# A graph attention kernel on one core: a transposed-attribute ring of 8 instead of 3, rings of 3 for the sums, gathered pieces handed back one by one

## The chip, the cores and the metric

The kernel runs on one core of one Trainium2 chip. The metric is the device time of one execution in microseconds. The median of several executions is compared.

## The reference

One graph attention layer (8 heads of 16) with a residual, over 6250 nodes and 206250 edges sorted by destination:

```
h   = relu(layernorm(x))                                  # x [6250, 256]
xm  = h @ W_n2m.T;  ea = edge_attr @ W_r2m.T              # [6250, 128], [206250, 128]
xl  = xm @ Wl.T + bl;  xr = xm @ Wr.T + br
u   = leaky_relu(xl[src] + xr[dst] + ea @ We.T, 0.2)      # one row per edge, and one loop per node
logits = einsum(u as (edge, head, 16), att)
alpha  = softmax of the logits over the edges of one dst
out = segment_sum(xl[src] * alpha, dst) + bias
return x + out @ W_m2n.T
```

A node's loop edge has the mean of its edges' attributes.

## The kernel before, in words

The kernel has three parts. The **prologue** normalises x, writes the table `xl` to HBM, keeps `xr` in SBUF as three bf16 parts, and builds tables on the chip. One of them is `free_tab`: for each entry the value of `msg_ready` at which places of the ring of gathered rows are free again. The **edge loop** is what the change is about. The **finale** adds the loop edges, divides by the sums and projects.

The edges are cut into 806 pieces of 256. A step takes two pieces (512 edges), and there are 427 steps, since a piece that crosses a window of 128 nodes is walked twice. All engines walk the same steps, each in its own order, and meet by semaphores alone. Logits, maxima and weights are made for batches of 8 steps, so that the weighted sums of a step (its aggregation) come `LAG = 18` steps behind its logits. In iteration k:

- **SP** issues `slot_bc` for step k+2 (L777), reads the step's piece numbers from a table (L101), issues two `attrT` DMAs for step k (transposed attributes, 32 rows by 512 edges, L786), then two `rbf` DMAs for step k-17 (L794). Before `attrT` it waits for `z_done` of step k-TRING, before `slot_bc` for the one-hot of step k-2, before `rbf` for the copy of four steps earlier. Once in a batch it issues masks (L768).
- **GpSimd** gathers `xl` rows by source into `xl_g`, a ring of 64 pieces, two gathers per piece (L811). From piece 64 on it waits once per `FREED = 2` pieces on `msg_ready` against a value of `free_tab`.
- **TensorE** makes z of step k in one PSUM bank of two: six matmuls with the one-hot of destinations (L832), the attributes (L836, contraction over 32 rows), four transposes of the gathered rows (L840). Then the logits of step k-2 (L867), the aggregation of step k-18 (L881, `onehot` by `msg`) and, once a batch, transposes for maxima (L850, L856) and weights (L891). z of step k waits until u of step k-2 is made.
- **ScalarE** copies gathered rows to `xl_z` for step k+2 (L905), makes `onehot` of step k-17 (L927, L932), copies `rbf` into `msg` (L936), and makes the relu of z (L943).
- **VectorE** makes the one-hot of step k+2 (L983), `msg` of step k-17 (L1005 and L1010, which also signal `msg_ready`), adds the aggregation of step k-19 into `acc` (L1022, L1024), and makes u of step k (L1027). Its scans for the maxima follow in some iterations.

`onehot` and `msg` have two places each. So ScalarE's L932 and VectorE's L1005 of iteration k wait for `agg_done` of TensorE's iteration k-1. VectorE's L1022, behind L1005 in the same iteration, waits for that same aggregation.

Of the kernel before, what the change touches and what calls it, by code (L numbers as in the profile page):

```python
# [10 lines left out]
P = 128  # L11
# [3 lines left out]
TILES = 4  # L15
# [21 lines left out]
SRING = 4  # L37
TRING = 3
ARING = 4
PRING = 64  # L40
ZRING = 3
FREED = 2
FREE_ROW = 4
MRING = 2
UNROLL = 48
BATCH = 8
# [41 lines left out]
def inside(j, count):  # L88

    return not isinstance(j, int) or 0 <= j < count  # L90
# [92 lines left out]
def prologue(nc, banks, xl_table, slot_dram, masks_dram, inputs,  # L183
# [5 lines left out]
    with ExitStack() as ctx:  # L189
# [89 lines left out]
        col_ps = banks[:, 7, WALK // 2:WALK // 2 + CHUNKS * SPLIT]  # L279
        free_ps = banks[0:1, 3, 0:FREES]  # L280
        tab_ps = [banks[:, i].rearrange("p (t r) -> p t r", t=TILES) for i in range(2)]
# [178 lines left out]
        def _(pe):  # L460
# [24 lines left out]
            pe.wait_ge(met_ready, 1)  # L485
            nc.tensor.matmul(free_ps, ones[0:WINDOWS, 0:1], met[:], start=True, stop=True).then_inc(met_counted, 1)

# [24 lines left out]
            pe.wait_ge(tab_copied, CHUNKS)  # L512
            pe.wait_ge(free_ready, 1)
            for w, s, _ in sweep(pe, -1, WRING, WINDOWS - 2, WINDOWS, WRING, WRING):
# [18 lines left out]
        def _(dve):  # L533
# [64 lines left out]
            for to in (loads[:, 0:STEPS, 0:SPLIT], loads[:, LATE:, SPLIT:], by_step[:, 0:STEPS], sums[:, 0:STEPS, SPLIT:]):  # L598
                nc.vector.tensor_scalar(to, pieces[:, 0:STEPS], float(PIECES - 1), None, ALU.min).then_inc(tabs_ready, 1)
            dve.wait_ge(met_counted, 1)  # L600
            nc.vector.scalar_tensor_tensor(out=free_tab, in0=free_ps, scalar=TICK / SPLIT, in1=free_base[:],
                                           op0=ALU.mult, op1=ALU.add).then_inc(free_ready, 1)

# [57 lines left out]
def edge_loop(nc, banks, xl_table, slot_dram, masks_dram, attr_rows, attr_cols,  # L661
# [11 lines left out]
    with ExitStack() as ctx:  # L673
        def sb(name, shape, dt=FP32):
            return ctx.enter_context(nc.sbuf_tensor(name, shape, dt))
# [6 lines left out]
        masks = sb("masks", [P, MRING, MASKS], BF16)  # L682
        attrT = sb("attrT", [D_RBF, TRING, GROUP])
        xl_g = sb("xl_g", [P, PRING, PT, D_MSG])
# [3 lines left out]
        distance = sb("distance", [P, TILES, P])  # L688
        onehot = sb("onehot", [P, 2, TILES, P])
        msg = sb("msg", [P, 2, TILES, AGG])  # L690
        run_ends = sb("run_ends", [P, 4])
# [67 lines left out]
        def _(sp):  # L759
            for k, s, r in sweep(sp, -2, 4 * BATCH, STEPS - 2, STEPS + LATE, UNROLL, UNROLL):  # L760
# [21 lines left out]
                if inside(k, STEPS):  # L782
                    if inside(k - TRING, STEPS):
                        sp.wait_ge(z_done, k - TRING + 1)
                    for h in range(SPLIT):
                        sp.dma_start(attrT[:, s % TRING, h * PIECE:(h + 1) * PIECE],  # L786
                                     attr_cols[one(now[h])].rearrange("a k e -> (a k) e")
                                     ).then_inc(turned_in[s % TRING], 16)
# [31 lines left out]
        def _(pe):  # L820
            pe.wait_ge(set_up, SET_UP)
            for k, s, r in sweep(pe, first, *looped, last_turn, UNROLL, UNROLL):
                if inside(k, STEPS):
# [11 lines left out]
                    pe.wait_ge(turned_in[s % TRING], (r * (UNROLL // TRING) + s // TRING + 1) * FULL)  # L835
                    nc.tensor.matmul(z, Wc[0:D_RBF], attrT[:, s % TRING], start=False, stop=False)  # L836
                    pe.wait_ge(xl_ready, SPLIT * (k + 1))
# [33 lines left out]
                if inside(k - LAG, STEPS):  # L871
                    j = s - LAG
                    pe.wait_ge(msg_ready, TICK * (k - LAG + 1))
                    pe.wait_ge(attr_ready, TICK * (k - LAG + 1))
                    pe.wait_ge(oh_ready, TICK * (k - LAG + 1))
                    if inside(k - LAG - 2, STEPS):
                        pe.wait_ge(added, TICK * (k - LAG - 1))
                    for h in range(SPLIT):
                        for i in range(PT):
                            t = h * PT + i  # L880
                            mm = nc.tensor.matmul(U_ps[j % 2][:, h], onehot[:, j % 2, t], msg[:, j % 2, t],  # L881
                                                  start=i == 0, stop=i == PT - 1)
                    mm.then_inc(agg_done, 1)
# [14 lines left out]
        def _(act):  # L898
            for k, s, r in sweep(act, first, *looped, last_turn, UNROLL, UNROLL):
# [23 lines left out]
                if inside(k - LAG + 1, STEPS):  # L923
# [5 lines left out]
                    act.wait_ge(dist_ready, TILES * (k - LAG + 2))  # L929
                    if inside(k - LAG - 1, STEPS):  # L930
                        act.wait_ge(agg_done, k - LAG)
                    nc.scalar.activation(onehot[:, m % 2], distance[:], ACT.Relu, scale=-1.0, bias=1.0  # L932
                                         ).then_inc(oh_ready, TICK)
                if inside(k - LAG + 1, STEPS):
                    act.wait_ge(loads[m % ARING], (r * (UNROLL // ARING) + (s - LAG + 1) // ARING + 1) * FULL)
                    nc.scalar.activation(msg[:, m % 2, :, CNT:AGG],  # L936
                                         rbf[:, m % ARING].rearrange("p (t k) -> p t k", t=TILES), ACT.Copy
                                         ).then_inc(attr_ready, TICK)
# [22 lines left out]
        def _(dve):  # L961
# [5 lines left out]
            for k, s, r in sweep(dve, first, *looped, last_turn, UNROLL, UNROLL):  # L967
# [27 lines left out]
                if inside(k - LAG + 1, STEPS):  # L995
                    row = slice(m % BATCH * HEADS, (m % BATCH + 1) * HEADS)
                    if m % BATCH == 0:
                        b = r * (UNROLL // BATCH) + (s - LAG + 1) // BATCH
                        dve.wait_ge(wT_done, b + 1)
                    if inside(k - LAG - 1, STEPS):  # L1000
                        dve.wait_ge(agg_done, k - LAG)
                    to = msg[:, m % 2, :, 0:MSG].rearrange("p t (h c) -> p t h c", c=HC)
                    for h in range(SPLIT):
# [432 lines left out]
```

## Time and profile before

| | |
|---|---|
| median of 3 runs | 3236.71 us (3231.31 to 3242.29) |
| the profiled execution's own time | 3200.59 us |
| its span | 3198.8 us |
| busy share of the span: TensorE, VectorE, ScalarE, GpSimd | 78%, 46%, 49%, 51% |
| mean granted clock of TensorE | 0.828 |

The span runs from the first to the last instruction. "PE" is TensorE's matmuls, "PEld" its weight loads, "DVE" VectorE, "ACT" ScalarE, "POOL" GpSimd, "SPq" the queue of SyncE, which only issues DMAs. "issue" names idle time that ends with nothing that the profile shows, and "remote" a semaphore whose updater it cannot tell. The granted clock is 1.0 at 2.4 GHz and 0.5 at 1.2 GHz.

### The profile page before, as it was taken

The page shows a single profiled execution, that of the slowest core. Times are in us where ns is not written, and L with a number is a line of the kernel's source. Part 1 is how long each engine was busy: PE and PEld are TensorE (multiplying, and loading weights), DVE is VectorE, ACT ScalarE, POOL GpSimd, SP SyncE. Part 2 cuts the span into 40 slices and gives each one's busy share as a digit, 9 for nine tenths or more (in the row PEclk, how much of TensorE's full clock was granted, in tenths as well). Part 3 has the DMA queues.
Part 4 walks back from the last instruction along what each step waited for, and adds up shares of the span by engine and source line. Part 5 has one row for each costly group of instructions (what it writes and reads, how often), then busy time and mean ns, then how long its engine had stood idle before and what let it go on. Part 6 is the DMA issues. An engine that isn't in the chain of part 4 may idle for free. (4 is left out here: it accounts for less than half of the span.)

```text
span 3198.8 us, 62156 instructions
## 1 busy us (share of the span) xinstructions
PE 2501.8 (78%) x11639; PEld 1541.6 (48%) x11640; DVE 1470.5 (46%) x4279; ACT 1552.9 (49%) x4428; POOL 1631.7 (51%) x1819
## 2 busy tenths in 40 slices
PE   5613878888788888888887888878888878887987
PEld 3401545545455555445454555445554545444565
DVE  6401444444444444445444444444444444444577
ACT  3301545555455445445545455554545544544672
POOL 4874455555455455555555455555555555555203
PEclk9755988888888888878888788888888887888999
DMA  4221333333333333333333333333333333333317
GB/s 144 83 56 48 85 79 82 85 81 83 81 81 79 84 85 82 82 82 87 82 79 88 85 81 79 85 79 77 85 83 91 86 78 85 82 82 78 78 30 132
DMA packets 317109, 263.45 MB, mean 82 GB/s; under 512 B 173619, under 2 KB 289637, under 8 KB 316438
## 3 DMA queue, kind: packets, MB, share of 16 engines
q1 hardware_dynamic: 254222, 142.33, 17.1%
q0 software_dynamic: 57632, 113.02, 14.7%
q10 hardware_dynamic: 4840, 3.68, 0.4%
q8 instruction: 124, 2.03, 0.3%
q14 instruction: 291, 2.38, 0.3%
HBM read 247.39 MB, written 16.89 MB: 83 GB/s over the span
## 5 line engine op out<-in xcount | busy, mean ns | idle before, releaser
L811 POOL DMA_INDIRECT xl_g<-xl_table,src_tab x1612 | 1532.5, 951 | 1353.8 <-DVE msg L1010 871.7
L881 PE MATMUL banks<-msg,onehot 128*128 128x177 f32 x3416 | 771.9, 375 | 58.0 <-issue 51.7
L881 PEld LDWEIGHTS banks<-msg,onehot 128*128 128x128 f32 x3416 | 633.7, 226 | 265.7 <-issue 235.4
L1027 DVE SCALAR_TENSOR_TENSOR uT<-banks,uT 128x512 f32<-128x512 f32 x427 | 294.4, 689 | 922.1 <-ACT uT L943 480.5
L836 PE MATMUL banks<-attrT,Wc 32*128 32x512 f32 x854 | 548.2, 724 | 145.0 <-DMA attrT<-in_attr_cols 117.2
L927 ACT ACTIVATE distance<-iota_n,minus_slot 128x128 f32<-128x128 f32 x1708 | 550.4, 388 | 119.4 <-issue 119.1
L1005 DVE TENSOR_TENSOR msg<-xl_g,banks 128x256 f32<-128x256 f32 x854 | 320.8, 417 | 571.5 <-remote 409.6
L832 PE MATMUL banks<-onehotT,xr_parts 128*128 128x256 bf16 x2562 | 419.6, 303 | 196.1 <-issue 168.4
L943 ACT ACTIVATE uT<-banks 128x512 f32<-128x512 f32 x427 | 249.7, 585 | 648.4 <-remote 445.3
L905 ACT ACTIVATE xl_z<-xl_g 128x256 f32 x854 | 310.9, 407 | 224.2 <-issue 162.0
L932 ACT ACTIVATE onehot<-distance 128x512 f32<-128x512 f32 x427 | 269.0, 630 | 299.1 <-remote 164.1
L832 PEld LDWEIGHTS banks<-onehotT,xr_parts 128*128 x2562 | 270.3, 107 | 285.7 <-issue 217.8
L840 PEld LDWEIGHTS banks<-ident,xl_z 128*128 128x128 f32 x1708 | 203.2, 155 | 409.5 <-issue 363.3
L867 PE MATMUL banks<-uT,att_pad 128*64 128x256 f32 x1708 | 345.7, 474 | 31.2 <-issue 29.8
L840 PE MATMUL banks<-ident,xl_z 128*128 128x128 f32 x1708 | 320.8, 315 | 33.9 <-issue 33.0
L836 PEld LDWEIGHTS banks<-attrT,Wc 32*128 32x128 f32 x854 | 141.6, 206 | 262.1 <-DMA attrT<-in_attr_cols 136.2
L983 DVE TENSOR_SCALAR onehotT<-slot_bc,node_of 128x512 bf16<-128x512 bf16 x427 | 152.8, 358 | 81.9 <-issue 68.6
L1024 DVE TENSOR_TENSOR acc<-acc,banks 128x177 f32 x427 | 145.1, 340 | 73.6 <-issue 13.0
L867 PEld LDWEIGHTS banks<-uT,att_pad 128*64 128x64 f32 x1708 | 100.1, 153 | 120.9 <-issue 118.4
L1022 DVE TENSOR_TENSOR acc<-acc,banks 128x177 f32 x427 | 140.8, 330 | 5.2 <-issue 3.8
L936 ACT ACTIVATE msg<-rbf 128x128 f32<-128x128 f32 x427 | 126.5, 296 | 31.6 <-DMA rbf<-in_attr_rows 18.6
L856 PE MATMUL banks<-ones,end_row 1*128 1x1 f32 x216 | 40.8, 289 | 83.8 <-DVE end_row L1059 64.2
(199 smaller groups left out, 1430.3 us busy)
## 6 DMA issues: line engine op xcount, KB each, us to landing
slot_bc<-slot_dram SPq DMA_DIRECT2D x427, 128.0 KB
attrT<-in_attr_cols SPq DMA_DIRECT2D x854, 32.0 KB
rbf<-in_attr_rows SPq DMA_DIRECT2D x854, 32.0 KB
xl_g<-xl_table,src_tab POOLq DMA_INDIRECT x1612
masks<-masks_dram SPq DMA_DIRECT2D x108, 96.5 KB
out<-in_x SPq DMA_DIRECT2D x16, 336.0 KB
out<-result POOLq DMA_DIRECT2D x6, 896.0 KB, 8.4
xl_table<-lr_sb SPq DMA_DIRECT2D x49, 64.0 KB, 1.5
```

The lines of the kernel that those rows point to most:

```text
L811: pool.indirect_dma_start(out=xl_g[:, g % PRING, i], out_offset=None, in_=xl_table, in_offset=bass.IndirectOffsetOnAxis(ap=src_tab[:, j:j ...
L832: nc.tensor.matmul(z[:, h * PIECE:(h + 1) * PIECE], parts_of(xr_parts, w[h], part), onehotT[:, n4, h * PIECE:(h + 1) * PIECE], start=h == ...
L836: nc.tensor.matmul(z, Wc[0:D_RBF], attrT[:, s % TRING], start=False, stop=False)
L840: mm = nc.tensor.matmul(z[:, h * PIECE + i:(h + 1) * PIECE:PT], xl_z[:, s % ZRING, h, i], ident[:], start=False, stop=h == SPLIT - 1 and i ...
L867: mm = nc.tensor.matmul(LT_ps[par][h * ROWS:(h + 1) * ROWS], att_pad[:, ROWS - HEADS - i * HEADS:2 * ROWS - HEADS - i * HEADS], uT[:, n, h ...
L881: mm = nc.tensor.matmul(U_ps[j % 2][:, h], onehot[:, j % 2, t], msg[:, j % 2, t], start=i == 0, stop=i == PT - 1)
L905: nc.scalar.activation(xl_z[:, (s + 2) % ZRING, h].rearrange("p i d -> p (i d)"), xl_g[:, one(pieces[h] & (PRING - 1))].rearrange("p a i d ...
L927: nc.scalar.activation(distance[:, t], iota_n[:], ACT.Abs, bias=minus_slot[:, one(TILES * (k - LAG + 1) + t)]).then_inc(dist_ready, 1)
L932: nc.scalar.activation(onehot[:, m % 2], distance[:], ACT.Relu, scale=-1.0, bias=1.0).then_inc(oh_ready, TICK)
L943: nc.scalar.activation(uT[:, s % URING], z_ps[s % 2], ACT.Relu, scale=1.0 - SLOPE).then_inc(relu_ready, 1)
L1005: nc.vector.tensor_tensor(to[:, two, :, 0:D_HEAD], xl_g[:, one(pieces[h] & (PRING - 1))].rearrange("p a i (h d) -> p (a i) h d", d=D_HEAD) ...
L1027: nc.vector.scalar_tensor_tensor(out=uT[:, s % URING], in0=z_ps[s % 2], scalar=SLOPE, in1=uT[:, s % URING], op0=ALU.mult, op1=ALU.add).the ...
```

## The change

Three things change in the edge loop, and one in the prologue follows from them.

- `attrT` has 8 places instead of 3. They lie four to a column range, on 32 partitions each, so L836 takes its operands from partitions 0, 32, 64 or 96 on, with a tile position to match. `Wc` holds the same weights four times already.
- `onehot` and `msg` have 3 places instead of 2: L932 and L1005 wait for the aggregation one iteration earlier than before.
- `FREED` is 1: GpSimd waits and counts per piece, and reads four entries of `free_tab` per 4 pieces instead of per 8.
- `free_tab` so has 808 entries instead of 404: its count is made by two matmuls into two banks and two VectorE operations, and the comparison `met` is twice as wide.

```
-TRING = 3
+TRING = 8
+TROWS = P // D_RBF
...
-FREED = 2
+FREED = 1
...
+SUM_RING = 3
...
-        free_ps = banks[0:1, 3, 0:FREES]
+        free_ps = banks[0:1, 2:4, 0:FREES // 2]
...
-            nc.tensor.matmul(free_ps, ones[0:WINDOWS, 0:1], met[:], start=True, stop=True).then_inc(met_counted, 1)
+            for i in (0, 1):
+                nc.tensor.matmul(free_ps[:, i], ones[0:WINDOWS, 0:1], met[:, i * (FREES // 2):(i + 1) * (FREES // 2)],
+                                 start=True, stop=True).then_inc(met_counted, 1)
...
-            dve.wait_ge(met_counted, 1)
-            nc.vector.scalar_tensor_tensor(out=free_tab, in0=free_ps, scalar=TICK / SPLIT, in1=free_base[:],
-                                           op0=ALU.mult, op1=ALU.add).then_inc(free_ready, 1)
+            for i in (0, 1):
+                half = slice(i * (FREES // 2), (i + 1) * (FREES // 2))
+                dve.wait_ge(met_counted, i + 1)
+                nc.vector.scalar_tensor_tensor(out=free_tab[:, half], in0=free_ps[:, i], scalar=TICK / SPLIT,
+                                               in1=free_base[:, half], op0=ALU.mult, op1=ALU.add).then_inc(free_ready, 1)
...
-        attrT = sb("attrT", [D_RBF, TRING, GROUP])
+        attrT = sb("attrT", [P, TRING // TROWS, GROUP])
...
-        onehot = sb("onehot", [P, 2, TILES, P])
-        msg = sb("msg", [P, 2, TILES, AGG])
+        onehot = sb("onehot", [P, SUM_RING, TILES, P])
+        msg = sb("msg", [P, SUM_RING, TILES, AGG])
...
+                    to = slice(s % TROWS * D_RBF, (s % TROWS + 1) * D_RBF)
                     for h in range(SPLIT):
-                        sp.dma_start(attrT[:, s % TRING, h * PIECE:(h + 1) * PIECE],
+                        sp.dma_start(attrT[to, s % TRING // TROWS, h * PIECE:(h + 1) * PIECE],
...
-                    nc.tensor.matmul(z, Wc[0:D_RBF], attrT[:, s % TRING], start=False, stop=False)
+                    of = slice(s % TROWS * D_RBF, (s % TROWS + 1) * D_RBF)
+                    nc.tensor.matmul(z, Wc[of], attrT[of, s % TRING // TROWS], start=False, stop=False,
+                                     tile_position=(s % TROWS * D_RBF, 0))
...
-                    if inside(k - LAG - 1, STEPS):
-                        act.wait_ge(agg_done, k - LAG)
-                    nc.scalar.activation(onehot[:, m % 2], distance[:], ACT.Relu, scale=-1.0, bias=1.0
+                    if inside(k - LAG + 1 - SUM_RING, STEPS):
+                        act.wait_ge(agg_done, k - LAG + 2 - SUM_RING)
+                    nc.scalar.activation(onehot[:, m % SUM_RING], distance[:], ACT.Relu, scale=-1.0, bias=1.0
...
-                    if inside(k - LAG - 1, STEPS):
-                        dve.wait_ge(agg_done, k - LAG)
-                    to = msg[:, m % 2, :, 0:MSG].rearrange("p t (h c) -> p t h c", c=HC)
+                    if inside(k - LAG + 1 - SUM_RING, STEPS):
+                        dve.wait_ge(agg_done, k - LAG + 2 - SUM_RING)
+                    to = msg[:, m % SUM_RING, :, 0:MSG].rearrange("p t (h c) -> p t h c", c=HC)
```

## Rows read from the trace of the kernel before

**Rows 1.** The page: busy us, share of the span and instructions of each engine.

```profile
PE 2501.8 (78%) x11639; PEld 1541.6 (48%) x11640; DVE 1470.5 (46%) x4279; ACT 1552.9 (49%) x4428; POOL 1631.7 (51%) x1819
```

**Rows 2.** Windows by stage: us, busy and instructions per engine, clock, DMA share, GB/s.

```profile
110.00:300.00 190.00, 44.66 (x126) 19.92 (x124) 16.97 (x37) 11.24 (x27) 132.58 (x148) 0.52 0.23 59
...
400.00:2950.00 2550.00, 2089.81 (x9688) 1275.48 (x9685) 1163.80 (x3431) 1299.13 (x3760) 1345.02 (x1420) 0.83 0.33 82
```

**Rows 3.** Waits of TensorE, 400 to 2950 us: total us, times, longest.

```profile
PE banks L836 <- DMA attrT<-in_attr_cols: 117.2, 42, 11.1
...
PE banks L856 <- DVE end_row L1059: 58.9, 14, 6.5
...
PE banks L891 <- DVE msg L1010: 38.7, 21, 4.7
```

**Rows 4.** Waits of SyncE's queue, 400 to 2950 us.

```profile
SPq L786 <- remote: 62.6, 14, 10.1
SPq L786 <- PE banks L840: 16.0, 6, 6.3
SPq L794 <- ACT msg L936: 1.1, 1, 1.1
SPq L777 <- DVE onehotT L983: 0.3, 2, 0.2
```

**Rows 5.** Timeline of a late `attrT`: start us, us, engine, line, what.

```profile
1739.31 0.01 SPq L777 DMA_DIRECT2D slot_bc<-slot_dram  x1
...
1742.04 0.33 SPq L777 DMA_DIRECT2D slot_bc<-slot_dram  x1
...
1754.36 0.34 SPq L777 DMA_DIRECT2D slot_bc<-slot_dram  x1
...
1755.50 0.86 SPq L786 DMA_DIRECT2D attrT<-in_attr_cols  x2
...
1758.06 2.07 PE L836 MATMUL banks<-attrT,Wc 32*128 32x512 f32 x2 [3.87 <-DMA attrT<-in_attr_cols]
```

**Rows 6.** Timeline, same stretch: first and last of a run of 8 gathers, and next.

```profile
1741.20 0.94 POOL L811 DMA_INDIRECT xl_g<-xl_table,src_tab  x1 [3.48 <-DVE msg L1010]
...
1749.93 0.94 POOL L811 DMA_INDIRECT xl_g<-xl_table,src_tab  x1 [0.30 <-issue]
...
1754.55 0.94 POOL L811 DMA_INDIRECT xl_g<-xl_table,src_tab  x1 [3.67 <-DVE msg L1010]
```

**Rows 7.** Waits of GpSimd, 400 to 2950 us.

```profile
POOL xl_g L811 <- DVE msg L1010: 780.7, 184, 11.4
```

**Rows 8.** Waits of VectorE before `msg`, 400 to 2950 us.

```profile
DVE msg L1005 <- remote: 383.3, 96, 6.7
```

**Rows 9.** Timeline while GpSimd fills its ring: a relu long after its z.

```profile
157.55 1.12 PE L840 MATMUL banks<-ident,xl_z 128*128 128x128 f32 x4
...
184.78 0.60 ACT L943 ACTIVATE uT<-banks 128x512 f32<-128x512 f32 x1 [26.17 <-remote]
```

**Rows 10.** Timeline: two steps of TensorE at the full clock.

```profile
1512.71 1.47 PE L881 MATMUL banks<-msg,onehot 128*128 128x177 f32 x8
...
1514.02 0.82 PE L832 MATMUL banks<-onehotT,xr_parts 128*128 128x256 bf16 x6
...
1514.77 1.12 PE L836 MATMUL banks<-attrT,Wc 32*128 32x512 f32 x2
...
1515.82 0.66 PE L840 MATMUL banks<-ident,xl_z 128*128 128x128 f32 x4
...
1516.98 1.47 PE L881 MATMUL banks<-msg,onehot 128*128 128x177 f32 x8
```

**Rows 11.** Timeline of the prologue: the table of free places.

```profile
28.69 1.50 PE L486 MATMUL banks<-met,ones 49*1 49x404 f32 x2
...
32.86 3.67 DVE L599 TENSOR_SCALAR tabs<-walk 1x854 int32<-1x854 f32 x4
...
36.57 0.57 DVE L601 SCALAR_TENSOR_TENSOR tabs<-banks,free_base 1x404 int32<-1x404 f32 x1
```

More of the change, by code:

```diff
@@ L512, in _ @@
             pe.wait_ge(tab_copied, CHUNKS)
-            pe.wait_ge(free_ready, 1)
+            pe.wait_ge(free_ready, 2)
             for w, s, _ in sweep(pe, -1, WRING, WINDOWS - 2, WINDOWS, WRING, WRING):
@@ L880, in _ @@
                             t = h * PT + i
-                            mm = nc.tensor.matmul(U_ps[j % 2][:, h], onehot[:, j % 2, t], msg[:, j % 2, t],
+                            mm = nc.tensor.matmul(U_ps[j % 2][:, h], onehot[:, j % SUM_RING, t], msg[:, j % SUM_RING, t],
                                                   start=i == 0, stop=i == PT - 1)
@@ L935, in _ @@
                     act.wait_ge(loads[m % ARING], (r * (UNROLL // ARING) + (s - LAG + 1) // ARING + 1) * FULL)
-                    nc.scalar.activation(msg[:, m % 2, :, CNT:AGG],
+                    nc.scalar.activation(msg[:, m % SUM_RING, :, CNT:AGG],
                                          rbf[:, m % ARING].rearrange("p (t k) -> p t k", t=TILES), ACT.Copy
```

## The prediction

> **What bounds the kernel now.** I read the page first. TensorE is busiest at 78%, and nothing else passes 51% [rows 1]. The windows then split the time. The stretch from 400 to 2950 us, the steady edge loop, is 2550 of the 3198.8 us: TensorE is busy 2089.81 us there at a granted clock of 0.83, and GpSimd 1345.02 us [rows 2]. With 6.78 us per step (2550 us over about 376 steps, which are the 1420 gathers of that row by 3.775 per step: 1612 over 427) this is where a ring can matter.
>
> TensorE is not a plain bound. It idles 460 us there (2550 less 2089.81). The waits say for what. The largest is the one this change aims at: 117.2 us in 42 waits for `attrT` at L836. Behind it come 58.9 us for VectorE's scans (L856) and 38.7 us for `msg` (L891) [rows 3]. Clock 0.83 between two levels, 0.5 and 1.0, means that a third of the time TensorE runs at 1.2 GHz.
>
> So why is `attrT` late? If the ring of 3 were the reason, SP would stand at L786 until a place came free. It does so 20 times, for 62.6 + 16.0 = 78.6 us, and waits for nothing else (1.4 us) [rows 4]. The rest of its 2550 us SP is passing instructions, and the timeline shows at what pace. From one `slot_bc` to the next it takes 2.73 us when GpSimd is quiet (1739.31 to 1742.04), but 12.32 us (1742.04 to 1754.36, with a pair of mask loads in it) when GpSimd issues a run of eight gathers [rows 5, 6]. After that one the `attrT` of the stalled step is issued at 1755.50 and L836 starts at 1758.06, 3.87 us late [rows 5]. Gathers at 1.25 us each (0.94 and 0.30 between, [rows 6]) are 3.775 x 1.25 = 4.7 us of each step. SP does 4.7/12.3 = 0.38 of a step in them, and the other 0.62 takes 0.62 x 2.73 = 1.7 us: 6.4 us, next to the 6.78 us of a step. SP has hardly any slack. A longer ring can give it only the time in which it now stands, not a faster pace.
>
> GpSimd itself is not the bound: 780.7 us it waits for VectorE to free places [rows 7]. But its runs of gathers hold up others. While it fills its ring (110 to 300 us), TensorE is busy 44.66 of 190 us [rows 2], and a z that ends at 158.67 is taken up by ScalarE only at 184.78, after 26.17 us of "remote" [rows 9]. In the steady loop the same shows as VectorE's 383.3 us of "remote" before `msg` [rows 8]: TensorE's signal reaches it late.
>
> **The change part by part.**
>
> *attrT ring of 8.* It removes the wait at L786, up to 78.6 us of SP's time [rows 4]. What is late next: SP of iteration k then waits for the one-hot of step k-2 (L777) and the copy of `rbf` four steps back. These let it run about four steps ahead instead of two, so six of the eight places serve nobody. TensorE gets back from its 117.2 us [rows 3] no more than SP gains, since both sides are one queue: the stall comes where SP's lead is zero, the wait where it is two. Lower bound: nothing (at the late `attrT` in [rows 5] SP was behind by its own pace, not by the ring). Upper bound: 78.6 us. With a lead that wanders between 0 and 4 instead of 0 and 2, the ends are met about half as often. I take half: -39 us. The number of DMAs, of waits and of SP's instructions per step stays the same.
>
> *L836 in four row groups.* Two matmuls of 0.5 us and two weight loads per step, as before, over 32 rows. Cost taken: 0. The Trainium skill, TensorEngine Tiling (Array Packing), Key Properties, speaks against it: changing the tiling mode drains TensorE. By that rule, if the explicit tile position is a mode that L836 was not in, the matmul before and the one behind would each be waited out. What the rows show on either side: L832 ends at 1514.84 while L836 starts at 1514.77, and L836 ends at 1515.89 while L840 starts at 1515.82 [rows 10]. So there is 0.07 us of overlap on each side to lose: 0.14 x 427 = 60 us at most.
>
> *onehot and msg rings of 3.* L1005 no longer waits for the aggregation of iteration k-1, on which 383.3 us [rows 8] stand. But L1022, next on VectorE, waits for the same one, so the idle time moves behind `msg` and does not vanish. What becomes earlier is `msg`, hence `msg_ready`, by about the 1 us that L1005 and L1010 take: for TensorE's L891, which waits 38.7 us in 21 waits, at most 21 us, and for L856, 14 waits [rows 3], at most 14 us. ScalarE's L932 likewise stands before its L943. Behind it SP's `rbf` wait is already 1.1 us [rows 4]. Since SP has no slack to follow a faster TensorE, I take 0 of these 35 us and keep them as the range's lower side.
>
> *FREED of 1.* GpSimd waits on 742 pieces instead of 371 pairs and reads its table twice as often. The sequencer is ahead of the gathers within a run, where they stay 0.30 us apart [rows 6], so these instructions are hidden by the 0.94 us of a gather. If that cover were gone, 371 more waits at such a gap of 0.30 us would be 111 us, and GpSimd has 780.7 us of waiting to take them from [rows 7]. The two pieces of a step are freed by L1005 and L1010 within half a microsecond, and GpSimd needs 2.5 us per piece. It gives neither time nor more even runs: 0.
>
> *Prologue.* One more pair of matmuls (1.50 us), one more L601 (0.57 us), and a `met` twice as wide (404 columns more, by L599's 0.92 us for 854: 0.4 us) [rows 11]. Together 2.5 us, partly under other work on both engines; I take +2 us, with 0 and 2.5 as bounds.
>
> Sum: -39 + 0 + 0 + 0 + 2 = -37 us on the profiled execution's 3200.59 us, a factor of 0.9884. The median of the runs shown is 1.1% above that execution. The factor on the median, 3236.71, gives **3199 us**. Its own range, from 0 to -78.6 - 35 us: 3122 to 3239.
>
> **The rivals.**
>
> *The lead is not what SP lacks.* SP is late by its pace. The 20 waits give their time back and it is lost at the next late signal, because L777 ties SP to VectorE, which itself waits for TensorE's late signals. For it: [rows 5], where a place was free long before 1755.50. Against it: 78.6 us are real. It gives -9 to +9 us, 3228 to 3246, say 3238.
>
> *Longer runs of gathers (the other side).* `msg` now goes out before the wait for the aggregation. So places come free while TensorE's signal is still held back, GpSimd adds four gathers (5.0 us) to the run, and the signal is held back for as long. TensorE can go on for two steps only, by its two z banks: 2 x 4.27 us at the full clock (L881 at 1512.71 and 1516.98 [rows 10]). The run of 8 gathers, 10 us, just exceeds that; one of 12 stalls it another 5 us. The ring's 37 us are used up when 8 of the 1420/8 = 178 runs get longer (8 x 5 = 40). With 18 of them it is 90 - 37 = +53 us, a factor of 1.0166: 3290. I take the middle of 3246 and 3290, about 3270. For it: [rows 9], where a relu stands 26 us behind its z in an unbroken run. Against it: four gathers per step are freed whatever the order, so longer runs must also be rarer.
>
> *The stalls took the clock with them.* If the 42 stalls vanish, so does the slow clock behind them. A step at 1.2 GHz has L836 at 2.07 us against 1.12 [rows 5, 10], so by that ratio its 4.27 us grow by 3.6 us. 117.2 + 42 x 3.6 = 268 us less, a factor of 0.916: 2966; with half the stalls gone, 3101. The Trainium skill, TensorE: Matmul & The Clock Gate, says that the slow clock is the idle state and sustained activity releases it; clock 0.83 at 82% busy [rows 2] agrees. Against it: SP must supply the steps.
>
> *A drain at every L836.* +60 us by the rows above, less the 37 gained: +23 us, 3260; without the gain 3297.
>
> **How the numbers follow.** Forecast (a gain of 0.3 to 2.5%) 0.43; clock comes back too 0.09; no lead gained 0.23; longer runs 0.21; drain 0.04. A measurement of this kernel tells 0.3%, 10 us, from no change. Faster 0.43 + 0.09 = 0.52, less what of the forecast's own range lies within 10 us, 0.02: 0.50. Same 0.23 + 0.02 = 0.25. Slower 0.21 + 0.04 = 0.25. The range ends at 3120 on the fast side, at the forecast's own lower bound and short of the clock rival's 3101, and at 3272 on the slow side, so that the longer-runs rival is in it up to its middle. What is left out is some 0.09 and 0.11.
>
> **What would show it.** Right: the `attrT` wait at L836 falls from 117.2 to about 60 us; SP's waits at L786 are gone, and short ones appear at L777; VectorE's idle time moves from L1005 to L1022; L891's wait shrinks; L836 starts no later after L832. No lead gained: the `attrT` wait stays near 117 us. Longer runs: GpSimd shows runs of 12 and more, and TensorE waits at L832 for u. Clock: granted clock over 0.87 in the loop. The prediction is wrong if SP's pace is no property of the gathers but of its own waiting, or if VectorE's earlier `msg` changes the rhythm of the gathers.

## The result and the profile after

The change is slower: 3365.76 us median (3341.29 to 3372.72, 4 runs) against 3234.01 us (3206.04 to 3242.29, 4 runs: the three shown above and one more), a ratio of 1.0404 with a 95% interval of [1.0362, 1.0445]. The forecast was 3199 us, with a range from 3120 to 3272. The profiled execution has a span of 3361.9 us, 163.1 us more than before.

The page's first line of the kernel after, engines and busy time, against [rows 1]:

```profile
PE 2572.0 (77%) x11641; PEld 1569.3 (47%) x11642; DVE 1468.0 (44%) x4280; ACT 1553.4 (46%) x4428; POOL 1633.4 (49%) x1819
```

VectorE, ScalarE and GpSimd are busy for as long as before, within 3 us, so they only wait longer. TensorE is busy 70 us more for the same instructions, at a lower granted clock. The windows of the kernel after, against [rows 2]:

```profile
110.00:300.00 190.00, 45.41 (x129) 20.49 (x128) 17.04 (x37) 11.38 (x28) 132.81 (x150) 0.52 0.22 60
...
400.00:2950.00 2550.00, 2036.08 (x9140) 1230.47 (x9140) 1095.42 (x3237) 1226.71 (x3548) 1267.87 (x1337) 0.81 0.30 78
```

In equal time GpSimd issues 1337 gathers in place of 1420: a step takes 7.20 us, not 6.78. Nothing changed while the ring fills (45.41 against 44.66 us). So the loss is in the steady loop. Its waits, kernel after (line numbers moved: L832 is now L839, L836 L844, L840 L849, L856 L865, L881 L890, L891 L900; L1005 and L1010 are L1014 and L1019, L1022 L1031, L1027 L1036; L943 is L952, L811 L818; L768 L774, L777 L783, L794 L801. In the experiments below they lie a few lines off too, and the name of what is written says which is meant):

```profile
PE banks L839 <- issue: 156.0, 95, 3.2
PE banks L865 <- DVE end_row L1068: 75.7, 25, 6.4
...
PE banks L900 <- DVE msg L1019: 44.7, 23, 2.9
...
DVE uT L1036 <- ACT uT L952: 684.6, 165, 9.1
DVE acc L1031 <- remote: 301.3, 37, 11.6
...
DVE msg L1014 <- remote: 51.4, 12, 5.8
...
ACT uT L952 <- remote: 560.2, 92, 9.5
...
POOL xl_g L818 <- DVE msg L1019: 897.7, 169, 8.7
...
SPq L774 <- DVE run_max L1088: 27.6, 16, 2.3
SPq L783 <- DVE onehotT L992: 23.4, 23, 2.7
SPq L801 <- ACT msg L945: 0.2, 1, 0.2
```

Three things are to be seen. The wait that the forecast lived on, L836 for `attrT` [rows 3], is no longer among the waits, nor is SyncE's for a place [rows 4]. VectorE no longer stands at `msg` (383.3 us of "remote" in [rows 8], now 51.4) but at `acc` (301.3) and at uT (684.6, before 407.2 as shown below). And GpSimd waits 897.7 us for `msg`, 117 us more than in [rows 7]. The line of the kernel before, VectorE's waits, 400 to 2950 us:

```profile
DVE uT L1027 <- ACT uT L943: 407.2, 109, 9.7
```

One cycle shows how these hang together. Timeline of the kernel after, all engines in order of time:

```profile
1735.34 0.94 POOL L818 DMA_INDIRECT xl_g<-xl_table,src_tab  x1 [5.70 <-DVE msg L1019]
...
1740.82 2.73 PE L890 MATMUL banks<-msg,onehot 128*128 128x177 f32 x8
...
1741.50 0.22 DVE L1019 COPY msg<-banks 128x64 f32<-128x64 f32 x1
...
1745.36 0.66 PE L849 MATMUL banks<-ident,xl_z 128*128 128x128 f32 x4
...
1749.23 0.95 POOL L818 DMA_INDIRECT xl_g<-xl_table,src_tab  x1 [0.30 <-issue]
...
1752.81 0.60 ACT L952 ACTIVATE uT<-banks 128x512 f32<-128x512 f32 x1 [7.76 <-remote]
1752.89 0.34 DVE L1031 TENSOR_TENSOR acc<-acc,banks 128x177 f32 x1 [11.16 <-remote]
...
1753.63 0.69 DVE L1036 SCALAR_TENSOR_TENSOR uT<-banks,uT 128x512 f32<-128x512 f32 x1
...
1756.83 0.75 DVE L1014 TENSOR_TENSOR msg<-xl_g,banks 128x256 f32<-128x256 f32 x2
...
1757.49 0.23 DVE L1019 COPY msg<-banks 128x64 f32<-128x64 f32 x1
...
1758.02 0.95 POOL L818 DMA_INDIRECT xl_g<-xl_table,src_tab  x1 [7.85 <-DVE msg L1019]
```

A run of 12 gathers lasts from 1735.34 to 1750.18. TensorE ends an aggregation at 1743.55 and a z at 1746.02, but both signals reach VectorE and ScalarE at 1752.8, 2.7 us after the run. The trace has the updates of these two semaphores themselves at 1752.67 and 1752.79 us. So it is the signals that are late, and not the engines that wait for them. VectorE has already written the next `msg` (L1019 at 1741.50) and stands at `acc`. Before GpSimd can start again, VectorE must do `acc`, uT, the work of a batch, the one-hot and the next `msg`: 7.85 us without a gather. In [rows 6] that gap is 3.67 us, with VectorE standing at `msg` itself.

The Trainium skill, Perfetto Trace Analysis, Per-instruction lifecycle, says that the propagation of a semaphore lies outside the recorded slices. This trace agrees: no row holds the 6.8 us from the end of L849 to L952, it appears as "remote" alone.

### The profile page after: what moved, and what is told of

Its sections match the earlier page's. It is cut to its first block and busy times, and to the rows that moved or that the text cites. A ratio compares the mean times of both kernels' runs of the same rounds, so it can differ in the third digit from the quotient of the medians.

```text
span 3361.9 us, 62601 instructions
## 1 busy us (share of the span) xinstructions
PE 2572.0 (77%) x11641; PEld 1569.3 (47%) x11642; DVE 1468.0 (44%) x4280; ACT 1553.4 (46%) x4428; POOL 1633.4 (49%) x1819
## 5 line engine op out<-in xcount | busy, mean ns | idle before, releaser
L818 POOL DMA_INDIRECT xl_g<-xl_table,src_tab x1612 | 1533.9, 952 | 1514.5 <-DVE msg L1019 1054.7
L890 PE MATMUL banks<-msg,onehot 128*128 128x177 f32 x3416 | 788.3, 380 | 88.1 <-issue 83.1
L1036 DVE SCALAR_TENSOR_TENSOR uT<-banks,uT 128x512 f32<-128x512 f32 x427 | 294.6, 690 | 1136.4 <-ACT uT L952 805.6
L890 PEld LDWEIGHTS banks<-msg,onehot 128*128 128x128 f32 x3416 | 644.4, 229 | 295.0 <-issue 245.3
L952 ACT ACTIVATE uT<-banks 128x512 f32<-128x512 f32 x427 | 250.4, 586 | 1053.2 <-remote 772.3
L839 PE MATMUL banks<-onehotT,xr_parts 128*128 128x256 bf16 x2562 | 441.6, 309 | 297.2 <-issue 277.9
L844 PE MATMUL banks<-attrT,Wc 32*128 32x512 f32 x854 | 559.5, 736 | 42.8 <-issue 42.7
L839 PEld LDWEIGHTS banks<-onehotT,xr_parts 128*128 x2562 | 276.3, 109 | 406.7 <-issue 333.1
L849 PEld LDWEIGHTS banks<-ident,xl_z 128*128 128x128 f32 x1708 | 206.8, 157 | 428.9 <-issue 356.7
L876 PE MATMUL banks<-uT,att_pad 128*64 128x256 f32 x1708 | 357.0, 477 | 46.0 <-issue 45.6
L849 PE MATMUL banks<-ident,xl_z 128*128 128x128 f32 x1708 | 327.6, 319 | 40.8 <-issue 29.9
L1031 DVE TENSOR_TENSOR acc<-acc,banks 128x177 f32 x427 | 142.0, 333 | 483.5 <-remote 350.8
L1014 DVE TENSOR_TENSOR msg<-xl_g,banks 128x256 f32<-128x256 f32 x854 | 320.7, 416 | 59.9 <-remote 53.0
L844 PEld LDWEIGHTS banks<-attrT,Wc 32*128 32x128 f32 x854 | 144.0, 208 | 160.0 <-issue 153.8
L865 PE MATMUL banks<-ones,end_row 1*128 1x1 f32 x216 | 45.8, 312 | 99.5 <-DVE end_row L1068 92.0
```

What stands on the lines that cost most here:

```text
L818: pool.indirect_dma_start(out=xl_g[:, g % PRING, i], out_offset=None, in_=xl_table, in_offset=bass.IndirectOffsetOnAxis(ap=src_tab[:, j:j ...
L839: nc.tensor.matmul(z[:, h * PIECE:(h + 1) * PIECE], parts_of(xr_parts, w[h], part), onehotT[:, n4, h * PIECE:(h + 1) * PIECE], start=h == ...
L844: nc.tensor.matmul(z, Wc[of], attrT[of, s % TRING // TROWS], start=False, stop=False, tile_position=(s % TROWS * D_RBF, 0))
L849: mm = nc.tensor.matmul(z[:, h * PIECE + i:(h + 1) * PIECE:PT], xl_z[:, s % ZRING, h, i], ident[:], start=False, stop=h == SPLIT - 1 and i ...
L876: mm = nc.tensor.matmul(LT_ps[par][h * ROWS:(h + 1) * ROWS], att_pad[:, ROWS - HEADS - i * HEADS:2 * ROWS - HEADS - i * HEADS], uT[:, n, h ...
L890: mm = nc.tensor.matmul(U_ps[j % 2][:, h], onehot[:, j % SUM_RING, t], msg[:, j % SUM_RING, t], start=i == 0, stop=i == PT - 1)
```

## The experiments

All kernels below have one addition: the numbers read from tables are ANDed (`& 2047`, `& 1023`) before GpSimd and ScalarE wait on them. The kernel before that each ratio compares with has no AND. `m_before` is the kernel before with that alone. The theories:

- **A, the gate.** The rings of 3 let `msg` go out before VectorE waits for the aggregation. That changes when GpSimd's runs start, and carries the whole loss.
- **B, SyncE.** The ring of 8 lets SyncE run far ahead, and its transfers or its waits in another order cost the time.
- **C, single pieces.** Giving back piece by piece costs GpSimd time.

### The parts one by one

The kernel before on this chip: 3233.49 us.

`m_before`: 3246.99 us, 1.0032 [0.9999, 1.0066].

> The kernel before, where each value read from a table is bounded by an AND with a constant (2047 for msg_ready, 1023 for landed) before it is waited for; the experiments that follow have the same ANDs. One register operation more per step on ScalarE, one per piece pair on GpSimd: all theories expect within 0.3% of before.

`m_ring8`: `TRING = 8` with its row groups, alone.

> The attrT ring of 8 alone. Theory A (the earlier msg changes the rhythm of the gathers and carries the whole loss of 4.0%): 0 to 1.2% faster than before. Theory B (SP far ahead carries it: its DMAs then go out beside the gathers, and TensorE's signals reach ScalarE later): 3 to 4% slower, and ScalarE's remote wait at its relu, 336.4 us before and 598.7 us after, is up here too. Theory C (handing back single pieces): as A here.

Measured: 3244.68 us, 1.0025 [0.9982, 1.0069]. `m_sum3`: `SUM_RING = 3` with the earlier waits of VectorE and ScalarE, alone.

> The rings of 3 for onehot and msg alone. Theory A: 3 to 4% slower, with runs of 12 gathers more often. Theories B and C: within 0.5% of before, with VectorE's idle time moved from L1005 to L1022.

Measured: 3414.49 us, 1.0536 [1.0482, 1.0591]. `m_freed1`: `FREED = 1` with its prologue, alone.

> The pieces handed back one by one alone, with the table for it. Theory C: 3 to 4% slower. Theories A and B: within 0.3% of before, 2 us of prologue.

Measured: 3222.38 us, 0.9965 [0.9931, 0.9999]. As single causes B and C fall, and the rings of 3 alone lose at least as much as the whole change (5.4% against 4.0%, and against 4.5% for the same change measured again below). What gives the difference back is open: neither the ring of 8 nor the single pieces were run on top of the rings of 3 alone. With rings of 3 alone SyncE comes to stand for a place. Windows and SyncE's waits of `m_sum3`, 400 to 2950 us:

```profile
400.00:2950.00 2550.00, 2033.74 (x8982) 1222.86 (x8980) 1075.17 (x3174) 1206.44 (x3480) 1243.37 (x1316) 0.79 0.30 76
...
SPq L787 <- remote: 165.5, 45, 10.3
SPq L787 <- PE banks L841: 85.2, 26, 11.4
```

These 250.7 us cost TensorE nothing directly: in `m_sum3`, with its `attrT` ring of 3, none of TensorE's waits is for `attrT`. So the wait of [rows 3] goes away without the ring of 8.

With the ring of 8 alone SyncE hardly waits for a place, and L836 waits for `attrT` as much as before. ScalarE's "remote" wait at its relu, which theory B expected to rise, is 223.8 us against 258.9 in `m_before`. (Of the two values in the expectation 598.7 is up to 3100 us; up to 2950 us it is 560.2.) The same stretch of `m_before`, then of `m_ring8`:

```profile
PE banks L836 <- DMA attrT<-in_attr_cols: 192.0, 72, 7.6
...
SPq L786 <- remote: 20.8, 4, 10.0
SPq L786 <- PE banks L840: 11.3, 3, 8.1
```

```profile
PE banks L839 <- DMA attrT<-in_attr_cols: 183.8, 74, 9.3
...
SPq L788 <- remote: 0.7, 1, 0.7
```

### Which wait, and is it GpSimd's start?

The kernel before on this chip: 3229.23 us. `s3_dve_old` has rings of 3, with this edit in VectorE's stream:

```
-                    if inside(k - LAG + 1 - SUM_RING, STEPS):
-                        dve.wait_ge(agg_done, k - LAG + 2 - SUM_RING)
+                    if inside(k - LAG - 1, STEPS):
+                        dve.wait_ge(agg_done, k - LAG)
```

> Rings of 3 for onehot and msg, but VectorE still waits for the previous aggregation before it writes msg, as before the change; only ScalarE's earlier wait before onehot is used. Against the kernel with rings of 3 alone, 3414 us. The gate theory: the loss comes from msg_ready being raised, and GpSimd's next run of gathers started, while TensorE's signals are still under way; with VectorE's old wait the next run starts as before, so the loss is gone: 3225 to 3265 us, the waits of ScalarE's relu for TensorE in all 400 to 2950 us back near 420 us, GpSimd's gathers near 1400 in that stretch. The rival, that ScalarE's earlier onehot puts ScalarE in another order against its relu: the loss stays, 3380 to 3420 us. A second rival, that a third buffer costs by its place in memory alone: the loss stays too.

Measured: 3247.44 us, 1.0112 [1.0012, 1.0213]. `s3_act_old` is the same edit in ScalarE's stream instead.

> The mirror of the kernel before it: rings of 3, ScalarE keeps the old wait for the previous aggregation before onehot, VectorE alone writes msg early. The gate theory: the whole loss stays, 3385 to 3425 us, with GpSimd's runs as in rings of 3 alone. The rival of ScalarE's order: the loss is gone, 3225 to 3265 us. If each of the two kernels carries a part, both theories have a share and the parts are read from the two ratios.

Measured: 3419.46 us, 1.0624 [1.0535, 1.0714]. So VectorE's early `msg` is the carrier. ScalarE's early one-hot and the third buffer as such are not, though the interval of `s3_dve_old` leaves them up to 2.1%; `s3_added`, which keeps both, is at 1.0058. `s3_added` has both early waits, and at GpSimd

```
-                    pool.wait_ge(msg_ready, freed[g // FREED % FREE_ROW] & 2047)
+                    pool.wait_ge(added, freed[g // FREED % FREE_ROW] & 2047)
```

> Rings of 3 and both early waits, and one word changed at GpSimd: before it reuses a piece it waits for `added` (VectorE's two additions to acc, which follow the aggregation) in place of msg_ready, with the same counts. The ring of 64 pieces holds 16 steps more than the piece in use, so nothing is held back for want of a buffer beyond one step. The gate theory: GpSimd's runs start again behind TensorE's signal, and the loss is gone, 3210 to 3265 us, though msg is still early. The rival of ScalarE's order, and the rival of the third buffer's place in memory: 3380 to 3420 us. A third possibility, that a gate one step later leaves the piece ring short: over 3300 us with ScalarE waiting for landed.

Measured: 3239.96 us, 1.0058 [1.0016, 1.0099]. `msg` is as early as in `m_sum3`, only GpSimd starts behind the aggregation again, and 5% of loss become 0.6%. The same count of `added` comes two iterations after that of msg_ready, since VectorE adds step k-19 where it makes `msg` of step k-17. That leaves GpSimd no shorter of room: ScalarE waits 33.1 us for gathered rows in `s3_added` and 51.7 us in `m_before`. Waits of `s3_added`, 400 to 2950 us:

```profile
PE banks L837 <- DMA attrT<-in_attr_cols: 189.8, 83, 6.9
...
POOL xl_g L812 <- DVE acc L1025: 809.4, 189, 13.6
...
DVE acc L1023 <- remote: 390.6, 85, 7.0
```

VectorE stands at `acc` as long as in `m_sum3` (385.5 us), so it is not that wait which costs, but what lies between it and GpSimd's next start. And as the loss goes, TensorE's `attrT` wait returns: 189.8 us, near the 192.0 of `m_before`. `b_added` is the kernel before with the same one word.

> The kernel before with rings of 2 and the same one word: GpSimd waits for `added` in place of msg_ready, so a run of gathers starts one operation of VectorE later (after the two additions, some 1.5 us behind msg). The gate theory in its strong form: what matters is how much of TensorE's and VectorE's chain lies between two runs, so this is 0 to 2% faster than before, 3170 to 3245 us. In its weak form (what matters is only that the run starts behind the aggregation's signal, and it does already): within 0.5% of before, 3225 to 3255 us. If GpSimd's own pace sets the step, 1.5 us later per step cannot be caught up: slower, 3280 us and more.

Measured: 3287.08 us, 1.0215 [1.0117, 1.0313]. Neither form of the theory was right: later is not better. The size is that of the third case. From VectorE's place at `msg` the two additions to `acc` now lie before GpSimd's start as well, and the gap that follows a stall there is 4.34 us in place of 3.58 (table below).

The account of all these comes from the gather records between 400 and 2950 us. Gathers less than 0.6 us apart are one run. The time per gather, times 1612, splits into that within runs and that between them. The last columns say at which of VectorE's instructions a run's end finds it, and the mean gap that follows:

```
kernel        runs  in runs   in gaps   span    at msg       at uT        at acc
before         212  1947 us    951 us   3198.8  114, 3.30 us  67, 5.44 us    0
m_before       221  1946       991      3228.8  125, 3.58     55, 5.27       5, 1.64 us
m_ring8        220  1944       994      3240.9  131, 3.64     48, 5.53       0
m_freed1       241  1941       974      3223.4
s3_dve_old     214  1951       972      3227.2  118, 3.47     55, 5.61       0
s3_added       212  1956       981      3237.7   21, 3.57     38, 5.31     110, 3.78
b_added        206  1962      1009      3279.2  121, 4.34     38, 5.38       3, 2.91
after          194  1951      1122      3361.9   29, 1.87     98, 5.55      37, 6.99
change_again   199  1943      1170      3394.9
s3_act_old     187  1949      1181      3416.7   27, 1.55     91, 5.76      37, 8.07
m_sum3         189  1945      1182      3415.5   29, 1.71     75, 5.81      47, 7.74
```

The time within runs is the same everywhere, within 21 us. So the gaps must grow with the span, which is arithmetic and proves nothing yet: 951 to 1122 is +171 us where the span grows by 163.1, and within one chip 991 (`m_before`) to 1182 (`m_sum3`) is +191 where it grows by 186.7. What tells the cause is the last columns. A run's end used to find VectorE at `msg`, 3.3 us from the next gather, in more than half of the cases. With the early `msg` it mostly finds it at uT or at `acc`, 5.5 to 8 us away.

Longer runs are not the main cost. Behind a run of 8 gathers the mean gap is 4.43 us in the kernel before, 5.27 in the one after and 5.82 in `m_sum3`; behind one of 12 it is 6.86, 7.38 and 8.03 us. Per gather a run of 12 has about as much gap as one of 8 (0.57 and 0.55 us in the kernel before). It is the gap behind runs of equal length that grew.

### Without the gathers, and on another chip

`plain_b` and `plain_s3` replace the gather of the edge loop:

```
-                pool.indirect_dma_start(out=xl_g[:, g % PRING, i], out_offset=None, in_=xl_table,
-                                        in_offset=bass.IndirectOffsetOnAxis(ap=src_tab[:, j:j + 1], axis=0),
-                                        engine_sem=landed).then_inc(landings[j % FLIGHT], 16)
+                pool.dma_start(xl_g[:, g % PRING, i], xl_table[0:P]).then_inc(landings[j % FLIGHT], 16)
+                pool.sem_inc(landed, 1)
```

These two and `t8f1` and `all_added` ran on a chip on which the kernel before itself took 2293.43 us (2290.75 to 2299.24), not 3230.

> The kernel before, with each of the 1708 indirect gathers replaced by an ordinary DMA of the same 64 KB from 128 fixed rows of the table, issued by GpSimd at the same place under the same waits. It leaves out the gather itself: the rows are the wrong ones, so its output is not the reference's; all other work is the same. All theories: GpSimd is no longer busy 0.95 us per piece, TensorE's signals are not held back, and the time falls to between TensorE's busy time of 2572 us with its issue gaps and 2950 us. If it stays above 3100 us, the gathers were never what lengthens the step, and the gate theory falls as a whole.

Measured: 2200.0 us median, 0.9593 [0.9577, 0.9609], from four runs of 2199.33 to 2205.00 us. A fifth, the one with the trace, took 4903.28 us with TensorE busy 99% of its span. Why is open, and nothing here rests on that trace.

> Rings of 3 for onehot and msg, with the same replacement of the gathers as in the kernel before it, and the same part of the work left out. The gate theory: without gathers there is nothing to start too early, so rings of 3 cost nothing: within 0.5% of plain_b, or up to 2% faster, since VectorE may run ahead. The rival, that the third ring costs by itself (order of VectorE and ScalarE, place of the buffers in memory): 4 to 6% slower than plain_b, as rings of 3 were against before.

Measured: 2195.46 us (2194.56 to 2196.58), 0.9566 [0.9552, 0.9581]: rings of 3 cost nothing without the indirect gathers. But this chip can't say that the gathers were the reason, since the loss of the rings of 3 was never shown on it. `t8f1` is the whole change without rings of 3.

> The whole change without rings of 3: attrT as a ring of 8 in four row groups, and pieces given back one by one. Single pieces alone measured 0.9965 and the ring of 8 alone 1.0025 against the kernel before. If they add, 0.996 to 1.001, 3215 to 3240 us. If the ring of 8 is worth something only when the runs of gathers are shorter (SyncE then is held less), 0.985 to 0.995. If the three parts only lose together, about 1.00.

Measured: 2294.93 us, 1.0004 [0.9995, 1.0013]. `all_added` is the whole change with GpSimd waiting for `added`.

> The whole change with one word more: GpSimd waits for `added` in place of msg_ready before it reuses a piece. The gate theory: the change's loss of 4% is gone, and it stands as rings of 3 with the same wait (1.0058) plus what single pieces give: 0.998 to 1.010, 3225 to 3262 us. If the loss of the whole change has another cause than that of rings of 3 alone, it stays above 1.02.

Measured: 2291.70 us, 0.9988 [0.9979, 0.9997]. The sizes expected were for the other kind of chip. Here nothing distinguishes the kernels, and the trace says why. Timeline of `t8f1` while GpSimd fills its ring, against [rows 9]:

```profile
186.55 0.94 POOL L817 DMA_INDIRECT xl_g<-xl_table,src_tab  x1 [0.30 <-issue]
...
186.57 0.66 PE L848 MATMUL banks<-ident,xl_z 128*128 128x128 f32 x4
187.13 0.58 ACT L951 ACTIVATE uT<-banks 128x512 f32<-128x512 f32 x1
...
187.80 0.94 POOL L817 DMA_INDIRECT xl_g<-xl_table,src_tab  x1 [0.30 <-issue]
```

Within an equally unbroken run of equally long gathers the relu starts as its z ends. In [rows 9] it starts 26 us later. From 110 to 2050 us of `t8f1` 134 relus found ScalarE idle, and none of them started more than 0.12 us behind its z. Windows of `t8f1`:

```profile
110.00:300.00 190.00, 154.33 (x676) 81.08 (x675) 77.96 (x205) 75.85 (x217) 144.43 (x161) 0.76 0.41 103
400.00:2050.00 1650.00, 1610.17 (x8994) 1017.49 (x8992) 1088.83 (x3186) 1197.92 (x3497) 1248.20 (x1319) 0.98 0.47 118
```

TensorE is busy 154.33 of 190 us while the ring fills (44.66 in [rows 2]), and 98% of the steady loop at a granted clock of 0.98. It is the bound, so the start of a run should decide nothing.

The last two ran on a chip of the slower kind again, the kernel before at 3244.79 us. `change_again` is the whole change.

> The whole change once more, without anything undone. The gate theory says that the loss needs gathers that hold TensorE's signals back. So: on a chip where the kernel before takes about 2290 us, TensorE is the bound, the start of GpSimd's runs decides nothing, and this is 0.995 to 1.003 of before. On a chip where the kernel before takes about 3230 us: 1.035 to 1.050, as measured before. The rival, that early msg or the third ring costs by itself whatever the gathers do: 1.03 or more on a chip of either kind.

Measured: 3396.99 us, 1.0453 [1.0399, 1.0506], as on the first chip. `plain_again` is the kernel of `plain_s3`.

> Rings of 3 for onehot and msg with the indirect gathers replaced by ordinary DMAs of the same bytes from fixed rows; it leaves the gather itself out, so the output is not the reference's. Measured once on a chip where the kernel before takes 2293 us: 2195 us. The gate theory, on a chip where the kernel before takes about 3230 us: the two kinds of chip differ only in what a running gather does to the signals, so without gathers this takes 2190 to 2230 us there too, 0.68 to 0.69 of before. If the slower kind of chip is slower for another reason (its clock, its memory), it stays above 2600 us. On a chip of the faster kind: 2195 us again.

Measured: 2203.66 us, 0.6776 [0.6739, 0.6813]. Page of `plain_again`, engines, and GpSimd's group of part 5:

```profile
PE 2105.7 (96%) x11639; PEld 1340.0 (61%) x11640; DVE 1461.5 (66%) x4279; ACT 1563.0 (71%) x4428; POOL 955.2 (43%) x1819
...
L812 POOL DMA_DIRECT2D xl_g<-xl_table x1612 | 855.9, 539 | 1030.7 <-DVE msg L1010 952.7
```

Without the indirect gathers the slower kind of chip is within 0.4% of the quicker kind's 2195.46 us, rings of 3 and all. So the two kinds differ in what a running gather does to the rest of the kernel. The late signals are the part of it that the traces show; whether there is another was not separated. That difference is worth some 950 us (3244.79 less 2293.43), the clock that TensorE loses with its stalls included: it is busy 2105.7 us here and 2501.8 in [rows 1], for the same matmuls.

What was not run: the whole change on the quicker kind (`all_added` there has the later start of GpSimd, so its 0.9988 does not stand for it), `plain_b`, `t8f1` and `all_added` on the slower kind. That one word takes the loss away is thus shown for the rings of 3 alone, and for the whole change only argued. No kernel here that does the whole work beats the kernel before by more than `m_freed1`'s 0.35%.

## Why the prediction was wrong

**The step that failed** is the term "onehot and msg rings of 3", taken at 0 with a bound of 35 us of gain: "the idle time moves behind `msg` and does not vanish". It did move (383.3 us at `msg` to 301.3 at `acc`), but its new place is not equal to the old. GpSimd's next run starts on `msg`. Before, VectorE stalled directly in front of `msg`, so that little work lay between the end of the stall and GpSimd's start. Now it stalls behind one `msg`, and `acc`, uT and the one-hot lie between the end of the stall and the next. That work went into most of the gaps. Alone the term, taken at 0 to -35 us, measures +167 us against `m_before` (1.0536 and 1.0032 of the kernel before); in the whole change the span grew by 163 us, beside 171 us of longer gaps.

**What bounds the kernel** was read wrongly before that. "GpSimd itself is not the bound: 780.7 us it waits" is true and misleads. Runs of gathers hold most of the signals back, and the signals let the next run start. That closed loop sets the time on this kind of chip: 1947 us of runs and 951 us of gaps in a span of 3198.8 us. A wait inside such a loop is not slack.

**The rival "longer runs"**, given 0.21, had the cause (the early `msg`) and the side, but not the mechanism, and its price of +53 us was three times too small. Runs of 12 grew from 12 to 25 and the mean run from 8.1 to 8.3 us only. The price lay in the gaps, 3.96 to 4.78 us in the mean, and not in a stall of TensorE by a longer run. The last condition under which the prediction would be wrong, "if VectorE's earlier `msg` changes the rhythm of the gathers", is what happened.

**The ring of 8**, -39 us: its mechanism fell too. SyncE's wait at L786 vanishes (32.1 us in `m_before`, 0.7 in `m_ring8`), and the `attrT` wait stays (192.0 and 183.8 us), with 1.0032 and 1.0025 in time. That is the rival "the lead is not what SP lacks" (0.23) for this term. In the whole change the `attrT` wait is gone, but not by the ring of 8: it is gone in `m_sum3` too, with a ring of 3, and back in `s3_added`, where the loss is undone. A longer step is what these share: half the issues of `attrT` are 16.1 us or more ahead of their use in the kernel after and 12.0 in `m_sum3`, against 6.2 before and 4.1 in `s3_added`. The sign expected at L836 came true because the kernel around it was slower.

Two readings under this term were weak as well. The 78.6 us and 117.2 us are those of one trace; `m_before`, the same kernel but for the ANDs, has 32.1 and 192.0 us. And a SyncE that runs four steps ahead leaves at most four of eight places unused, not six.

**Row groups**, 0 us: right. The drain of the Trainium skill's TensorEngine Tiling (Array Packing), Key Properties, was priced at up to 60 us by the rows; `m_ring8`, which has the row groups, is 2 us below `m_before`. So no such drain shows; one of some 10 us would be hidden in the interval.

**FREED of 1**, 0 us: a small gain instead. Against `m_before` 24.6 us less, with gaps down by 17 us (991 to 974), and 241 runs in place of 221: "neither time nor more even runs" was off by that. **The prologue**, +2 us: the first gather starts at 119.82, before at 119.09, so +0.7 us. Single traces differ as much: `m_sum3`, without the longer table, has 118.54.

**The clock** did not come back, 0.83 to 0.81. On the slower kind of chip it falls with longer gaps (0.79 in `m_sum3`) and is 0.976 when the gathers are gone (`plain_again`). It goes with TensorE's stalls; no run changed one without the other.

## What to carry to other kernels

When an engine's stall moves, ask what stands behind it in that engine's program, and who waits for that. A stall of equal length at a later instruction can lengthen a loop that runs through another engine. Waiting time of an engine means slack only if its start doesn't depend on something that its own work delays. And a buffer more can make a kernel slower, by letting a producer release another engine's work too early; one word at the consumer's wait undid it for the rings of 3. Last, a wait that goes away is no gain by itself: look whether it also goes away in a slower kernel without the edit that was meant to remove it, as the one for `attrT` did here.

## What the chip showed beyond that

- While GpSimd issues indirect gathers back to back, TensorE's signals reach ScalarE and VectorE late, once by 26 us [rows 9], and mostly only when the run is over. The trace has the update of the semaphore behind that relu at 184.76 us, 0.02 us before it starts. In the kernel after, of the 114 relus of the steady loop that start over 2 us behind their z with ScalarE idle, 102 start outside a run, in the median 1.9 us after one. The rest start within one, so the hold is not complete (in the kernel before 24 of 69). On the chip where the kernel before took 2293 us it was absent, with gathers of the same length. Why the chips differ stays open.
- Ordinary DMAs issued by GpSimd, 539 ns of it each, don't do this on the slower kind of chip (2203.66 us).
- The Trainium skill, Trainium Architecture — The Big Picture, What this means for kernel authors, says that engines run independently unless a semaphore links them. The runs agree in the letter, but on the slower kind of chip a third engine's work delayed the semaphore itself, in a kernel that took some 950 us longer there than on the quicker kind.
